# State-space layers: residual added by TensorE, the gate behind the product with B, one combined weight for dt, ReLU last, B and C projected into another bank

## The reference

```
residual = hidden if residual is None else hidden + residual
h = rmsnorm(residual, norm_w)
u, z = split(h @ in_w)                      # 128 channels each
uc = silu(conv4(u) + cb)
x_dbl = uc @ xp_w                           # 16 dt columns, 16 of B, 16 of C
dt = softplus(x_dbl[:, :16] @ dt_w + dt_b)
state[s] = exp(dt * A[s]) * state[s] + dt * uc * B[s]      # s = 0..15, over the tokens
y = sum_s state[s] * C[s] + uc * D
hidden = (y * silu(z)) @ out_w
```

## Time and profile before

| | |
|---|---|
| median of 3 runs | 426.04 us (424.88 to 426.66) |
| the profiled execution | 426.97 us |
| its span, first to last instruction | 425.1 us |
| mean granted TensorE clock | 0.928 |
| busy: PE / DVE / ACT / POOL | 349.8 / 320.7 / 245.6 / 214.2 us |
| chain that ended last, by engine | PE 52%, DVE 26%, ACT 11%, issue 5%, DMA 3%, POOL 2% |
| its largest lines | PE L641 15%, DVE L1123 8% |

### The profile page before, as it was taken

The page is one execution under the profiler, slowest core; times in us unless marked ns, Lnnn a source line. Parts: engine busy times, 40 slices in busy tenths (PEclk is TensorE's granted clock), DMA queues, the critical chain, the costliest instruction groups (busy, mean ns, idle before and its releaser), DMA issues.

```text
span 425.1 us, 5816 instructions
## 1 busy us (share of the span) xinstructions
PE 349.8 (82%) x1778; PEld 242.7 (57%) x1778; DVE 320.7 (75%) x549; ACT 245.6 (58%) x673; POOL 214.2 (50%) x239
## 2 busy tenths in 40 slices
PE   4858899887969998788879888887988888786684
PEld 3346655555648565466657566665756666565452
DVE  2764788686744360888998999899899997999563
ACT  2001398575633646576785858678586876764061
POOL 2950740000000012868796878879797897774000
PEclk9996999999995989689998998999899998998868
DMA  7900000000000301431515062242506235050000
GB/s 246 377 2 1 0 2 0 2 1 2 0 2 0 93 9 40 162 122 77 195 46 199 5 238 84 115 148 91 199 2 238 80 121 197 4 201 1 0 2 12
DMA packets 11345, 35.24 MB, mean 83 GB/s; under 512 B 2368, under 2 KB 2992, under 8 KB 11192
## 3 DMA queue, kind: packets, MB, share of 16 engines
q1 hardware_dynamic: 11032, 34.61, 22.8%
q10 hardware_dynamic: 288, 0.33, 0.3%
HBM read 34.54 MB, written 0.39 MB: 82 GB/s over the span
## 4 chain that ended last, share of the span: by engine, by line
PE 52%; DVE 26%; ACT 11%; issue 5%; DMA 3%; POOL 2%; DVEq 0%; SPq 0%; POOLq 0%
PE PS L641 15%; DVE big L1123 8%; ACT PS L1381 3%; PE PS L492 3%; PE PS L620 3%; DVE big L1111 3%; DVE big L1130 3%; ACT sg L1344 2%; PE PS L632 2%; PE PS L291 2%; PE PS L604 2%; DVE big L888 2%; PE PS L552 2%; PE PS L384 2%; PE PS L463 2%
## 5 line engine op out<-in xcount | busy, mean ns | idle before, releaser
L1123 DVE TENSOR_TENSOR_SCAN big<-PS,big 128x1024 f32<-128x1024 f32 x48 | 109.3, 2286 | 2.6 <-ACT PS L1381 2.5
L641 PE MATMUL PS<-big,cst 128*128 128x256 f32 x384 | 97.5, 412 | 0.0
L1381 ACT ACTIVATE PS<-dt,amat 128x255 f32<-128x255 f32 x192 | 79.7, 463 | 25.5 <-DVE dt L1095 21.6
L1592 POOL TENSOR_TENSOR big<-dtu,big 128x1024 f32<-128x1024 f32 x36 | 84.2, 2354 | 7.7 <-DVE dtu L1098 5.5
L641 PEld LDWEIGHTS PS<-big,cst 128*128 128x128 f32 x384 | 77.9, 208 | 15.4 <-issue 3.7
L1625 POOL TENSOR_SCALAR lnv<-mv 128x4 f32<-128x4 f32 x1 | 0.4, 417 | 99.1 <-DVE mv L747 99.1
L1130 DVE TENSOR_TENSOR big<-big,PS 128x1024 f32<-128x1024 f32 x36 | 43.8, 1218 | 0.9
L1229 ACT ACTIVATE big<-PS 128x512 f32<-128x512 f32 (+1 forms) x39 | 22.9, 586 | 30.7 <-PE PS L492 14.4
L620 PE MATMUL PS<-stack,pick_b 96*128 96x256 bf16 x144 | 23.5, 289 | 17.7 <-DVE big L1130 9.8
L1269 ACT ACTIVATE big<-PS,big 128x256 f32<-128x256 f32 x64 | 29.6, 471 | 11.1 <-DVE big L879 11.1
L1600 POOL TENSOR_TENSOR big<-big 128x1024 f32<-128x1024 f32 x12 | 28.3, 2357 | 1.1 <-DVE big L1123 1.1
(11 more groups left out here) (301 smaller groups left out, 646.2 us busy)
## 6 DMA issues: line engine op xcount, KB each, us to landing
big<-spill SPq DMA_DIRECT2D x48, 512.0 KB, 5.5
wmt<-in_wm SPq DMA_DIRECT2D x6, 418.0 KB, 3.9
w3t<-in_w SPq DMA_DIRECT2D x1, 1588.0 KB, 13.1
big<-routed SPq DMA_DIRECT2D x8, 128.0 KB, 3.0
w2t<-in_w SPq DMA_DIRECT2D x1, 896.0 KB, 9.8
cst<-in_const SPq DMA_DIRECT2D x1, 848.0 KB, 7.7
w5t<-in_w SPq DMA_DIRECT2D x1, 812.0 KB, 14.7
w1t<-in_w SPq DMA_DIRECT2D x1, 385.0 KB, 8.1
```

The costliest lines, as they stand in the source:

```text
L641: last = pe.matmul(yps, ident, hc[:, g, s], start=False, stop=(g == NSG - 1 and s == SG - 1))
L1123: v.tensor_tensor_scan(flat(hst[g][:]), flat(da[g % 2]), flat(dbu[:, g]), 0.0, ALU.mult, ALU.add).then_inc(sem("m_h"), 1)
L1381: one = act.activation(da[g % 2][:, n, 1:N], dt[b][:, 1:N], ACT.Exp, scale=amat[k][:, col:col + 1])
L1592: pool.tensor_tensor(dbu[:, g], dtu[b][:].unsqueeze(1).to_broadcast([P, SG, N]), bsp[b][:, SG * (g - 1):SG * g], ALU.mult).then_inc(sem("m ...
```

## The change

- **Residual.** `carry` on TensorE writes the residual Y through the identity into the PSUM region of the out-projection, which then accumulates onto it. DVE's add goes. ACT takes the squares of the norm from PSUM and then copies the sum back into Y (`keep_residual`), and POOL's scale waits for that copy.
- **Gate.** DVE does the first product with B before the gate, not after it. TensorE spreads B before the last sum, behind a wait for the last product with C of the step before, and the last sum, `carry` and the out-projection follow.
- **dt.** At the start TensorE forms, for all six layers, the product of the two dt weights (six transposes, six products of 16 rows); ACT copies both results out. SP loads the raw weights with one transfer of 128 x 6 x 240 words and later, for layers 2 to 5, copies the combined weight from SBUF to SBUF behind each layer's weights. In a unit, dt's product reads uc directly and comes first.
- **B and C.** Their product goes to bank 0 in place of bank 7, 96 rows in place of 112; ACT sets the one column of that bank which must be zero again after the copy.
- **ReLU last.** ACT's order becomes Abs, Exp, the two copies of x_dbl, two Squares, the middle piece of the split, two Squares, the zero column, ReLU. ReLU waits for DVE's first polynomial step.
- **Polynomial.** DVE's second and later steps work in SBUF and no longer in PSUM.
- **POOL.** gz moves behind the split's last piece and waits for it.
- **Fillers.** One `keep_awake` matmul less in each unit; two groups of `spare` at the start are partly replaced by the new products.
- Increments of a semaphore that nobody waits for go (not shown), and two semaphores of one engine are merged.

```diff
@@ -190,6 +190,9 @@
 uc, gz, dt, dtu, yg = (two(n, [P, N]) for n in ("uc", "gz", "dt", "dtu", "yg"))
+wdt = sb("wdt", [P, NL, P])
+xp_raw = big[:, 20480:20480 + NL * (112 + P)].rearrange("p (n c) -> p n c", n=NL)
+xp_dt = big[:, 22016:22016 + NL * P]
@@ -206,7 +209,7 @@
 yps, idle_ps = PS[:, 6, 0:N], PS[:, 6, N:2 * N]
-ups, xd = PS[:, 7, 0:N], PS[0:112, 7, 0:N]
+ups, xd = PS[:, 7, 0:N], PS[0:96, 0, 0:N]
@@ -217,7 +220,7 @@
-    eng.wait_ge(sem(f"ld_wm{(s // 2) % 2}"), i * 16 + 16 * (s // 4 + 1))
+    eng.wait_ge(sem(f"ld_wm{(s // 2) % 2}"), i * 32 + 32 * (s // 4) + 16)
@@ -237,6 +240,8 @@
         sp.dma_start(wmt[k][:], wm[k]).then_inc(sem(f"ld_wm{k}"), 16)
+    at = WM.at["xp"][0]
+    sp.dma_start(xp_raw, wm[:, :, at:at + 112 + P].rearrange("n p c -> p n c")).then_inc(sem("ld_xp"), 16)
@@ -250,7 +255,9 @@
             sp.wait_ge(sem("m_hid"), 2 * n - 2)
+            sp.wait_ge(sem("m_wdts"), 3)
             sp.dma_start(wmt[n % 2][:], wm[n]).then_inc(sem(f"ld_wm{n % 2}"), 16)
+            sp.dma_start(wdt[:, n % 2], wdt[:, n]).then_inc(sem(f"ld_wm{n % 2}"), 16)
@@ -349,15 +356,27 @@
     last.then_inc(sem("f0_y"), 1)
-    spare(7, 4)
...
+    pe.wait_ge(sem("ld_xp"), 16)
+    for n in range(NL):
+        last = pe.transpose(PS[0:112, n // 4, (n % 4) * P:(n % 4 + 1) * P], xp_raw[:, n, 0:112], ident)
+    last.then_inc(sem("m_wdt"), 1)
+    spare(7, 3)
...
+    def dt_product(n):
...
+        return pe.matmul(PS[:, 5 - n // 4, (n % 4) * P:(n % 4 + 1) * P], xp_dt[96:112, n * P:(n + 1) * P],
+                         xp_raw[96:112, n, 112:112 + P], start=True, stop=True)
...
     to_T2(X, PS[:, 3, 0:N], "ln_out", 2, "turned")
-    spare(7, 1)
+    pe.wait_ge(sem("m_wdts"), 1)
+    for n in range(2):
+        dt_product(n)
...
         sem("g_pair"), 1)
-    spare(7, 3)
+    for n in range(2, NL):
+        last = dt_product(n)
+    last.then_inc(sem("m_wdt"), 1)
@@ -476,6 +495,7 @@
             if p == 0:
+                pe.wait_ge(sem("m_wdts"), 3)
@@ -594,14 +614,13 @@
-    def prep_x(u, k, b):
+    def prep_dt(u, k, b):
...
         pe.wait_ge(sem("m_zs"), u + 1)
-        pe.matmul(xd, WM.of(wmt[k], "xp"), uc[b][:], start=True, stop=True).then_inc(sem("m_xd"), 1)
...
-    def prep_dt(u, k, b):
-        pe.wait_ge(sem("m_xds"), u + 1)
-        pe.matmul(dtp, WM.of(wmt[k], "dtw")[96:112], xds[b][96:112], start=True, stop=True).then_inc(sem("m_dtp"), 1)
+        pe.matmul(dtp, wdt[:, k], uc[b][:], start=True, stop=True).then_inc(sem("m_dtp"), 1)
...
+    def prep_x(u, k, b):
+        pe.matmul(xd, WM.of(wmt[k], "xp")[:, 0:96], uc[b][:], start=True, stop=True).then_inc(sem("m_xd"), 1)
@@ -643,11 +662,17 @@
+    def carry(u, b, behind=True):
...
+        if behind:
+            pe.wait_ge(sem("m_dt"), u + 2)
+        pe.matmul(hidp, ident, Y[:, :, b], start=True, stop=False)
...
             last = pe.matmul(hidp[:, a], yg[b][:, a * P:(a + 1) * P], WM.of(wmt[k], "out"),
-                             start=True, stop=True)
+                             start=False, stop=(a == HALF - 1))
@@ -657,14 +682,16 @@
         if not first:
-            sum_y(u + -1, nb, NSG - 1)
+            pe.wait_ge(sem("m_hc"), u * 3)
...
         if not first:
+            sum_y(u + -1, nb, NSG - 1)
+            carry(u + -1, nb)
...
         if not last:
-            keep_awake(3)
+            keep_awake(2)
@@ -674,9 +701,8 @@
         if not last:
+            prep_dt(u + 1, nk, nb)
             prep_x(u + 1, nk, nb)
-        if not last:
-            prep_dt(u + 1, nk, nb)
@@ -687,16 +713,16 @@
     keep_awake(4)
+    prep_dt(0, 0, 0)
     prep_x(0, 0, 0)
-    keep_awake(1)
-    prep_dt(0, 0, 0)
-    keep_awake(5)
+    keep_awake(6)
...
         pe_step(0, s, last=(s == 11))
+    carry(UNITS - 1, 1, behind=False)
@@ -1074,25 +1100,20 @@
-    def residual(u, b):
-        v.wait_ge(sem("m_hid"), u + 1)
-        v.tensor_tensor(Y[:, :, b], Y[:, :, b], hidp, ALU.add).then_inc(sem("m_res"), 1)
...
-        for q in range(2, 4):
-            cq = quadratics()[q][2]
-            v.wait_ge(sem("m_q"), u * 4 + 4)
-            if q > 2:
-                v.wait_ge(sem("m_poly"), u * 3 + 1)
-            v.scalar_tensor_tensor(sp_u, sp_q[b][:, q], cq, sp_u, ALU.add, ALU.mult)\
-                .then_inc(sem("m_poly"), 1)
+        poly = sp_q[b][:, 2]
+        v.wait_ge(sem("m_q"), u * 4 + 4)
+        v.scalar_tensor_tensor(poly, poly, quadratics()[2][2], sp_u, ALU.add, ALU.mult).then_inc(sem("m_poly"), 1)
+        v.wait_ge(sem("m_poly"), u * 3 + 1)
+        v.scalar_tensor_tensor(poly, sp_q[b][:, 3], quadratics()[3][2], poly, ALU.add, ALU.mult)\
+            .then_inc(sem("m_poly"), 1)
...
         v.wait_ge(sem("m_poly"), u * 3 + 2)
-        v.tensor_tensor(sp_u, sp_u, sp_q[b][:, 0], ALU.mult).then_inc(sem("m_poly"), 1)
+        v.tensor_tensor(poly, poly, sp_q[b][:, 0], ALU.mult).then_inc(sem("m_poly"), 1)
...
         v.wait_ge(sem("m_relu"), u + 1)
-        v.tensor_tensor(dt[b][:], sp_u, sp_m[b][:], ALU.add).then_inc(sem("m_dt"), 1)
+        v.tensor_tensor(dt[b][:], poly, sp_m[b][:], ALU.add).then_inc(sem("m_dt"), 1)
@@ -1104,14 +1125,12 @@
         prep_dt(u, b)
-        if not first:
-            gate(u + -1, pk, nb)
...
         if not first:
-            residual(u + -1, nb)
+            gate(u + -1, pk, nb)
@@ -1151,8 +1170,8 @@
     gate(UNITS - 1, 1, 1)
-    residual(UNITS - 1, 1)
-    v.wait_ge(sem("m_res"), UNITS)
+    v.wait_ge(sem("m_hid"), UNITS)
+    chain(v.tensor_copy(Y[:, :, 1], hidp))
@@ -1255,6 +1274,11 @@
     root(2, 1, 2)
+    act.wait_ge(sem("m_wdt"), 1)
+    for n in range(2):
+        size = (4 - 2 * n) * P
+        one = copy(xp_dt[96:112, 4 * P * n:4 * P * n + size], PS[96:112, n, 0:size])
+    one.then_inc(sem("m_wdts"), 1)
@@ -1290,6 +1314,10 @@
+    act.wait_ge(sem("m_wdt"), 2)
+    for n in range(2):
+        copy(wdt[:, 4 * n:4 * n + 4 - 2 * n].rearrange("p n c -> p (n c)"), PS[:, 5 - n, 0:(4 - 2 * n) * P])\
+            .then_inc(sem("m_wdts"), 1)
@@ -1322,12 +1350,17 @@
         if ready is None:
-            act.wait_ge(sem("m_res"), u + -1)
+            act.wait_ge(sem("m_hid"), u + -1)
...
         for a in range(HALF):
-            act.activation(sqs[:, a], Y[:, a, b], ACT.Square, scale=D ** -0.5,
+            act.activation(sqs[:, a], hidp[:, a] if ready is None else Y[:, a, b], ACT.Square, scale=D ** -0.5,
...
+    def keep_residual(u, b):
...
+        act.wait_ge(sem("m_hid"), u + 1)
+        act.activation(Y[:, :, b], hidp, ACT.Copy).then_inc(sem("m_res"), 1)
@@ -1350,7 +1383,7 @@
         act.wait_ge(sem("m_xd"), u + 1)
-        act.activation(xds[b][0:112], xd, ACT.Copy).then_inc(sem("m_xds"), 1)
+        act.activation(xds[b][0:96], xd, ACT.Copy).then_inc(sem("m_xds"), 1)
@@ -1358,19 +1391,21 @@
         dtb = WM.of(wmt[k], "dtb")
-        act.activation(sp_u, dtp, ACT.Abs, bias=dtb).then_inc(sem("m_abs"), 1)
-        act.activation(sp_m[b][:], dtp, ACT.Relu, bias=dtb).then_inc(sem("m_relu"), 1)
-        act.wait_ge(sem("m_abs"), u + 1)
+        act.activation(sp_u, dtp, ACT.Abs, bias=dtb).then_inc(sem("m_u"), 1)
+        act.wait_ge(sem("m_u"), u * 2 + 1)
         act.activation(sp_u, sp_u, ACT.Exp, scale=-1.0).then_inc(sem("m_u"), 1)
-        act.wait_ge(sem("m_u"), u + 1)
+        prep_xd(u, k, b)
+        act.wait_ge(sem("m_u"), u * 2 + 2)
         for q, (kq, bq, _) in enumerate(quadratics()):
+            if q == 2:
+                act.wait_ge(sem("m_rest"), u + 1)
+                act.activation(stack[b][0:64], rest[0:64], ACT.Copy).then_inc(sem("m_mid"), 1)
...
-    def prep_middle(u, b):
...
-        act.wait_ge(sem("m_rest"), u + 1)
-        act.activation(stack[b][0:64], rest[0:64], ACT.Copy).then_inc(sem("m_mid"), 1)
+        act.wait_ge(sem("m_xds"), u + 1)
+        act.activation(PS[0:96, 0, 0:1], zero_t[0:96], ACT.Copy)
+        act.wait_ge(sem("m_poly"), u * 3 + 1)
+        act.activation(sp_m[b][:], dtp, ACT.Relu, bias=dtb).then_inc(sem("m_relu"), 1)
@@ -1395,6 +1430,8 @@
             prep_norm(u + 1, nk, nb, ("ln_norm", 7) if first else None)
+        if not first:
+            keep_residual(u + -1, nb)
@@ -1403,18 +1440,14 @@
         if not last:
-            prep_xd(u + 1, nk, nb)
             prep_softplus(u + 1, nk, nb)
-            prep_middle(u + 1, nb)
...
     prep_sig(0, 0, 0)
-    prep_xd(0, 0, 0)
     prep_softplus(0, 0, 0)
-    prep_middle(0, 0)
@@ -1533,17 +1566,19 @@
         pool.tensor_tensor(dmat[k][:], ident, WM.of(wmt[k], "d").to_broadcast([P, P]), ALU.mult)\
-            .then_inc(sem("consts0"), 1)
...
-    def prep_scale(u, b):
...
+    def prep_scale(u, b, first=False):
...
         pool.tensor_tensor(msq[b][:], ssq[b][:], eps_t[:].to_broadcast([P, 2]), ALU.add)\
-            .then_inc(sem("m_msq"), 1)
-        pool.wait_ge(sem("m_msq"), u)
+            .then_inc(sem("m_rms"), 1)
+        pool.wait_ge(sem("m_rms"), u * 2 + -1)
...
             .then_inc(sem("m_rms"), 1)
-        pool.wait_ge(sem("m_rms"), u)
+        pool.wait_ge(sem("m_rms"), u * 2)
```

(10 more changed lines are left out.)

22 lines of the change are left out of this document (11 added, 11 removed).

## The result

**The change made the kernel slower, by 0.9% in the ratio:** a median of 428.25 us (424.83 to 431.22, 20 runs) against 426.16 us of the kernel before on the same chip (421.61 to 428.92, 20 runs), a ratio of 1.009 with a 95% interval of 1.0063 to 1.0117. The ratios are formed without the runs that are more than 1.5% above the fastest of their kernel and are no quotients of the medians, which are of all runs. The two medians divide to 1.005, so the loss is 2.1 us by them and 3.8 by the ratio. Forecast were 422.2 us and "faster" as the likeliest outcome. The profiled execution took 429.68 us, its span 427.9.

A forecast was written before the change was run, and what follows sets the result against it. TensorE was taken to end every unit's last wait, its clock deciding how long. Units -5.1, half clock +0.9, start +0.4 and tail even gave -3.8 on the profiled 426.97, a median of 422.2 us; range 418 to 430.

The forecast's parts named there:

- S to U: In each unit, from the first scan's start (S) to uc's start (U): 8.5 us, squares starting 0.57 later.
- U to S: From uc's start to the next unit's first scan: 9.63 us, or 10.03 where POOL then scales weights (wcv).
- The steps: DVE polynomial steps with two SBUF inputs end no earlier than 0.27 us behind the POOL instruction they meet.
- Weights, the B broadcast and the later x_dbl: Weight transfers and B's broadcast costed at nothing; x_dbl copied later, yet POOL's product ends at U + 5.7, now 6.1.
- rival 1: DVE and POOL block each other in the units: periods of 18.5 and 19.0, time 426.8 us; chance 0.22.
- rival 2: Short polynomial steps do not collide with POOL; the last sum binds, units of 17.84, time 419.5 us; chance 0.20.
- rival 3: Half clock falls between S and U, 1.4 us per such unit; with six units 430.6 us; chance 0.15.
- The tail is even: At the kernel's end, the last add becomes a copy; no cost or gain.
- The opening: At the start, six transposes replace one spare, +0.4 us; six products replace four spares of the same length or more.
- -5.1 + 0.9: Eleven unit periods together gain 5.1 us; half clock in as many units as now costs 0.9.
- First uc to first S: Stretch from the first uc to the first scan, ahead of the eleven periods; the sum had no term for it.
- Half clock in as many units as now: Half clock over the units' sums stays as frequent as before, costing 4 x 0.1 + 0.5 = +0.9 us.

The follow-up runs named there:

- e12: The kernel after, unaltered, run again for a third profile; it took 430.06 us.
- e2: The kernel after with the polynomial back in PSUM and the ReLU back behind Abs; 433.45 us, ratio 1.0169 to the kernel before.
- e8: The kernel after with the gate put back ahead of the product with B and the last sum ahead of B's spread; 431.95 us, ratio 1.0163.
- e6: The kernel before with only the change's start: raw weights' transfer, six transposes, six products, copies, in place of four fillers; 426.4 us, ratio 1.0037.
- e13: The kernel after with the old opening; combined weights made behind the mixture of experts in place of two of seven fillers; 427.08 us, ratio 1.0045.
- e3: The kernel after with the opening's eight filler matmuls put back beside the transposes and products; 426.0 us, ratio 1.0052.
- e9: The kernel after with the polynomial in PSUM, three fillers per unit and the opening's eight fillers restored; 426.39 us, ratio 1.0016.
- e4: The kernel after with seven fillers added in the last unit behind its first group of sums; 427.7 us, ratio 1.001.
- e1: The kernel after, unaltered, run again; 426.72 us, ratio 1.0067 to the kernel before.
- e10: The kernel after with three fillers per unit in place of two; 429.46 us, ratio 1.0118.
- e5: The kernel before, unaltered, run again for its stages; no separate time given, its three profiled executions took 420.9 to 427.0 us.
- e7: The kernel before with only the gate moved behind the product with B and B spread ahead of the last sum; 429.76 us, ratio 1.0109.
- e11: The kernel before, unaltered, for a third profile; no separate time given, its three profiled executions took 420.9 to 427.0 us.
- e14: The kernel after with the old opening, combined weights made behind the mixture of experts, polynomial in PSUM, three fillers per unit; 426.46 us, ratio 1.0029.

## Why the prediction was wrong

**Right.** TensorE's last sum left the path and the alternation went. S to U 8.55 for 8.5. U to S 9.71 for 9.63, 10.26 for 10.03. The steps come where they were put: in the plain unit shown above POOL's product ends at U + 5.7, and DVE's steps at 6.0, 6.8 and 7.7 for 6.0, 6.72 and 7.53. Weights, the B broadcast and the later x_dbl cost nothing seen. None of the three rivals' signs is seen in full in the profiled execution: POOL's last piece grew from 0.66 to 0.72, which is a little of rival 1, though the periods of 18.3 and 18.8 lie half way to its 18.5 and 19.0; none of the three polynomial steps with two inputs in SBUF stayed at 0.42 (rival 2), and no half clock came between S and U behind the first unit (rival 3). But e12, the same kernel, has it once, for 2.3 to 2.4 us, and e2 and e8 twice each.

**The terms that failed.** The range of 418 to 430 held the 428.25, but by luck, for none of the forecast's or the rivals' ways led there: the units gave 2.6 us less than forecast, and the opening, the attention block, the first unit and the end, priced together at +0.4, took more than they had.

1. "The tail is even: its last add becomes a copy." It is not. The end is longer in every profile, by 2.0 us in the mean of three against three, of which 1.2 stand ahead of or in the DVE wait at the start of the last block and 0.84, which may be chance, behind it. I looked at the DVE instruction that changed and not at TensorE, which ends the last waits there: the residual's matmul stands ahead of the last sums (0.22), and the place of the half clock, harmless in all four profiles with the old units, reaches the last sums in seven of twelve with changed ones. The wait that is 0.39 longer is neither.
2. The opening: "+0.4", of which the layer norm's turn was the carrier. The six transposes took 1.49 for the 1.3 put down (a length for which I had no row), and T2a starts 0.03 later in the profiled pair and 0.3 in the mean of three, within its scatter. What cost was the next thing, the projections at half clock: 0.5 to 0.9, and, by the count of fourteen profiles, some 1.6 more in the attention block, 3.2 in the mean of three against three. For the attention block the sum had no term at all. I had written that the six products "replace four spares of the same length or more" and priced only their time, not what they do to the clock.
3. The units: -5.1 + 0.9 forecast, -1.6 in the mean of three (-2.5 in the profiled pair), with the two kernels' values overlapping (204.2 to 206.8 and 204.5 to 208.7). Periods of 18.3 and 18.8 for 18.13 and 18.53 make 6 x 0.17 + 5 x 0.26 = 2.3 of the difference. The rest is the base: the kernel before ran its units in 204.5 once, with four slow ones and no period above 19.7, and in 208.7 once.
4. First uc to first S, costed at nothing: the collisions happen there too, and nothing hides them: 9.49 for 8.95, +0.53. "Eleven periods" left the twelfth out.
5. "Half clock in as many units as now" was too dark: the units' clock rose from 0.95 to 0.98. Of the 0.9 that I had put down for it nothing was spent behind the first unit of the profiled execution, though one unit of e12 spent 2.4.

With 2.0 for the tail, 0.8 for the turn to the rotary work, 0.5 for the first unit and -1.6 for the units the sum is +1.7; with the attention block's 3.2 and the 0.7 around it the profiles come to +5.7, above the +2.1 of the medians and the 3.8 of the ratio. The turn, the attention block, the first unit and the tail are longer in all three profiles of the kernel after than in any of the kernel before; the units are shorter only in the mean. The split is from few profiles, and by the ratios, too, the parts are hard to tell apart: e6 (1.0037), e13 (1.0045) and the kernel after (1.009, 1.0067) have intervals that touch.

**By the page's rule.** The trace shows DVE's steps of 0.57 to 0.85 beside POOL and POOL's own instructions lengthened by 0.06, hbias from 0.19 to 0.37. The Trainium skill, "SBUF — State Buffer", "Who interferes with whom", calls the shared pair an exclusive lock: whoever issues first has it for the whole instruction and the other is blocked. DVE's half agrees: its steps end 0.28 or 0.29 behind POOL's. POOL's starts, 321.92 and 322.81, fall inside DVE's running steps (321.55 to 322.13 and 322.16 to 322.93), and yet it took only 0.06 longer than in the kernel before or, for gz, nothing: 0.72 in both kernels. The short hbias is nearer to the rule: it starts at 341.73, inside DVE's step of 341.20 to 342.05, and ends at 342.10, right behind it. Spans on POOL are rough, so POOL's half stays undecided here.

**What stays open.** How much of the attention block's extra time is the start's doing and by what link, since a full clock over the projections (e3, e9) did not take it away; whether the filler or chance keeps the half clock off U; what moves the half clock onto the last sums; and the 0.39 below.

## What to carry to other kernels

When a wait is taken off an engine in the loop's steady state, price the first and the last pass by themselves: there the covers are missing, and here the first pass and the end took 0.5 and 2.0 us where eleven passes won 1.6. Work that takes the place of filler matmuls on TensorE must be priced by what the next matmuls on the path then cost at half clock, and a filler put back must be counted too, if it stands ahead of the work on the path (e3, e4). A wait that was taken off the path can leave a half clock elsewhere that costs as much: two of them made e2's units 4.4 us longer. Take the base from several profiled executions where the clock falls on the path in some units: one can be 2 to 4 us off, as much as the gain looked for.

## What the runs showed of the hardware

A DVE wait grew by 0.39 us with nothing in the data flow to explain it. DVE's timeline of the kernel after, behind the last gate, then of e13:

```profile
400.29 0.28 DVE L1167 TENSOR_TENSOR hs<-Y,rowt 128x128 f32<-128x128 f32 x1
401.43 0.43 DVE L1178 TENSOR_TENSOR Z<-hs,small 128x256 f32<-128x256 f32 x1 [0.86 <-ACT small L1463]
```

```profile
397.65 0.28 DVE L1168 TENSOR_TENSOR hs<-Y,rowt 128x128 f32<-128x128 f32 x1
398.42 0.43 DVE L1179 TENSOR_TENSOR Z<-hs,small 128x256 f32<-128x256 f32 x1 [0.48 <-ACT small L1464]
```

ACT's result is there at 400.94 in the kernel after (0.20 from 400.74), and DVE starts 0.49 later. From the gate to this instruction it is 3.16 or 3.17 in nine profiles (after, e1 to e4, e8 to e10, e12); before, e5, e6, e7 and e11 have 2.77 or 2.78, and e13 and e14, whose DVE program is one wait longer far ahead of this place, 2.80. That would fit a cost that goes with where the instruction stands in DVE's program; but e13 and e14 change ACT's and TensorE's programs too. What it is, the traces don't say, and I have not tried it alone.

The length of a half-clock stretch in the last unit was of two kinds: 3 to 4 us in most profiles and about 10 in e2, e7, e10 and e13, where the granted clock is 0.50 from 5 us behind the last S until 15 us behind it. Windows of 1 us of e13:

```profile
382.00:383.00 1.00, 1.00 (x5) 0.79 (x4) 1.00 (x1) 0.00 (x0) 1.00 (x1) 0.60 0.00 0
...
391.00:392.00 1.00, 1.00 (x4) 0.82 (x3) 0.00 (x0) 0.00 (x0) 0.00 (x0) 0.50 0.00 0
392.00:393.00 1.00, 1.00 (x5) 0.83 (x5) 0.00 (x0) 0.00 (x0) 0.00 (x0) 0.78 0.00 0
```

(Its last S is at 377.47.) Nor is the place fixed by the code: the kernel after has the clock fall from 390.5 to 393.9 in one profile, 9.2 us behind its last S, and in e12 3.7 us behind it.
